# Second feed-forward stage of a fused attention kernel: groups of four pages taken in rounds of two

## What is computed

```
x = x + xattn(layernorm(x), ctx, ctx)        # 16 heads, causal
x = x + ffn_attn(layernorm(x))
# ffn_attn: q, k, v are each a "fast feed-forward" tree of the same input:
cur = 0                                       # 4 levels, 15 nodes, 16 leaves
for _ in range(4):
    cur = 2 * cur + 1 + (x . node_w[cur] + node_b[cur] >= 0)
leaf = cur - 15
y = relu(x @ w1[leaf] + b1[leaf]) @ w2[leaf] + b2[leaf]    # 256 -> 64 -> 256
# then softmax(q k^T / 16) v per batch
```

## Time and profile before

| | us |
|---|---|
| median of 3 executions | 640.76 (640.52 to 642.57) |
| profiled execution, its own time | 640.1 |
| its span in the profile | 638.3 |
| PE busy in the span | 586.1 (92%) |
| DVE / ACT / POOL busy | 439.1 / 299.0 / 236.9 |
| feed-forward stage, 425.3 to 551.8 | 126.5, PE busy 123.0, ACT 95.4, DVE 59.6, DMA share 0.97 |

### The profile page before, as it was taken

How to read it: one execution, slowest core, us unless ns; L and a number is a source line. 1 busy time by engine, 2 the same in 40 slices (tenths; PEclk the granted TensorE clock), 3 DMA queues, 4 the chain that set the end, 5 groups by cost and what they waited for, 6 DMA issues and landing times.

```text
span 638.3 us, 14744 instructions
## 1 busy us (share of the span) xinstructions
PE 586.1 (92%) x5131; PEld 494.5 (77%) x5131; DVE 439.1 (69%) x1511; ACT 299.0 (47%) x482; POOL 236.9 (37%) x298
## 2 busy tenths in 40 slices
PE   8677999999899999999999897859999999799996
PEld 7566888877788887888888686848888888689995
DVE  2765666988788898898898787873555555156664
ACT  4104544544444453554445355007877787533331
POOL 6700010143143243334323326660006666666551
PEclk9869999999899999999999899879999999999999
DMA  6798788898998898899898749977999999766653
GB/s 190 221 305 261 237 230 226 252 260 238 283 271 249 286 310 247 258 297 283 251 296 275 208 134 303 309 254 274 324 364 387 411 408 375 258 191 197 200 177 126
DMA packets 99639, 169.58 MB, mean 266 GB/s; under 512 B 12848, under 2 KB 67824, under 8 KB 99568
## 3 DMA queue, kind: packets, MB, share of 16 engines
q1 hardware_dynamic: 87712, 141.83, 70.5%
q0 software_dynamic: 9216, 25.18, 12.5%
q10 hardware_dynamic: 2640, 1.65, 0.9%
HBM read 92.59 MB, written 75.50 MB: 263 GB/s over the span
## 4 chain that ended last, share of the span: by engine, by line
PE 51%; DMA 26%; SPq 13%; DVE 5%; issue 3%; ACT 1%; POOL 1%; DVEq 0%; ACTq 0%; POOLq 0%
DMA parts_dram<-k_lo 9%; DMA k<-parts_dram 8%; PE banks L840 6%; PE banks L825 6%; PE banks L814 6%; DMA parts_dram<-q_lo 5%; SPq L334 5%; PE banks L882 4%; PE banks L903 4%; PE banks L530 4%; PE banks L545 4%; PE banks L557 3%; SPq L317 2%; PE banks L871 2%; PE banks L573 2%
## 5 line engine op out<-in xcount | busy, mean ns | idle before, releaser
L1537 POOL DMA_INDIRECT xs_dram<-xn2s,place x96 | 95.7, 997 | 159.4 <-ACT pt L936 142.4
L1174 DVE TENSOR_REDUCE mneg<-banks 128x2 f32<-128x512 f32 x240 | 121.8, 548 | 44.9 <-PE banks L546 43.8
L936 ACT ACTIVATE pt<-banks 128x768 f32<-128x768 f32 x128 | 103.5, 810 | 102.2 <-PE banks L558 101.7
L545 PE MATMUL banks<-k,q 107*128 107x256 f32 x240 | 76.4, 369 | 17.7 <-DMA k<-parts_dram 10.9
L557 PE MATMUL banks<-q,k 109*128 109x256 f32 x256 | 74.0, 341 | 2.0 <-DMA q<-m_lo 0.3
L545 PEld LDWEIGHTS banks<-k,q 107*128 107x128 f32 x240 | 46.5, 194 | 29.3 <-DMA k<-parts_dram 16.3
L558 PE MATMUL banks<-q,k 109*128 109x128 f32 x256 | 57.3, 224 | 0.0
L573 PE MATMUL banks<-pt,vp 128*32 128x256 f32 (+1 forms) x1024 | 56.4, 339 | 0.4 <-ACT pt L936 0.4
L1596 POOL DMA_INDIRECT q_all<-ys_dram,place x32 | 30.8, 964 | 67.1 <-DMA ys_dram<-yb 53.8
L546 PE MATMUL banks<-k,q 107*128 107x128 f32 x240 | 54.4, 227 | 0.0
L557 PEld LDWEIGHTS banks<-q,k 109*128 109x128 f32 x256 | 48.7, 190 | 6.8 <-ACT pt L936 5.7
(11 more groups left out here) (177 smaller groups left out, 1290.9 us busy)
## 6 DMA issues: line engine op xcount, KB each, us to landing
ys_dram<-yb SPq DMA_DIRECT2D x36, 512.0 KB, 6.2
xb<-xs_dram SPq DMA_DIRECT2D x35, 512.0 KB, 7.7
k<-parts_dram SPq DMA_DIRECT2D x128, 128.0 KB, 3.8
q<-parts_dram SPq DMA_DIRECT2D x64, 256.0 KB, 4.6
xs_dram<-zero SPq DMA_DIRECT2D x45, 256.0 KB
xs_dram<-zero SPq DMA_DIRECT2D x18, 384.0 KB, 4.8
tables<-leafw SPq DMA_DIRECT2D x16, 257.0 KB, 8.2
xt<-x SPq DMA_DIRECT2D x16, 256.0 KB, 4.9
```

What stands on the lines that cost most here:

```text
L545: mm(ps[:, 0:S], q[0:KN, t, P:S], k[0:KN, t, :], start=True, stop=True)
L936: nc.scalar.activation(pt[:, 2 * p:2 * p + 2, :], st_banks(b, p)[:, :, 0:S + P], ACT.Exp, scale=SC).then_inc(exp_sb, 1)
L1174: last = nc.vector.tensor_reduce(mneg[1 - u][:, t, 2 * j:2 * j + 2], S_BANKS[:, :, cols], axis=AX.X, op=ALU.max, negate=True)
L1537: gp.indirect_dma_start(xs_dram[tree], bass.IndirectOffsetOnAxis(ap=place[:, k:k + 1], axis=0), xn2s[m % RING][:, t, :], None).then_inc(sc ...
```

## The change

Quads are handled in rounds of two. On PE a round is now: transposes of q + 2 and q + 3, second layers of q and q + 1, first layers of q + 2 and q + 3 (before: one quad of each kind in turn). ACT and SP follow the same order: both `copy_xT`, both `copy_y`, both `relu`; two loads, two stores. The transposes alternate between `pairs[0]` and `pairs[1]`, and the first layers move to banks 4 and 5, which the second layer of even quads uses too; so `block_h` waits for the `copy_y` of the even quad before it, and `block_out` waits for both `relu` of the round. POOL's gathers are released by `after_sixth`, six points in a round of two. No instruction of the computation is added or taken away.

```
--- before.py
+++ after.py
@@ -483,12 +483,14 @@
                     scattered(sp, tree, m)
             for q in range(QB, QB + AHEAD):
                 load_quad(q)
-            for q in range(TREES * QUADB):
-                if q + QB + AHEAD < TREES * QUADB:
-                    load_quad(q + QB + AHEAD)
-                store_quad(q)
-                if q in TABLE2:
-                    load_table(2, 2 + TABLE2.index(q))
+            for q in range(0, TREES * QUADB, 2):
+                for ahead in (q + QB + AHEAD, q + QB + AHEAD + 1):
+                    if ahead < TREES * QUADB:
+                        load_quad(ahead)
+                for done in (q, q + 1):
+                    store_quad(done)
+                    if done in TABLE2:
+                        load_table(2, 2 + TABLE2.index(done))
 
 
             def rows(ap, b):
@@ -806,30 +808,30 @@
                     pe.wait_ge(xb_first, 16)
                 else:
                     pe.wait_ge(xb_in[w], 16 * (q // QB + 1))
-                ge(pe, xbT_sb, q)
+                ge(pe, xbT_sb, q - 1)
                 for m in range(4):
                     if q == 0 and m == 2:
                         pe.wait_ge(xb_in[0], 16)
                     for c in range(C):
-                        last = nc.tensor.transpose(banks[c][:, m * P:m * P + P], xb[w][:, m, c * P:c * P + P], ident[:])
+                        last = nc.tensor.transpose(pairs[w % 2][:, c, m * P:m * P + P], xb[w][:, m, c * P:c * P + P], ident[:])
                 last.then_inc(xbT_ps, 1)
 
             def block_h(q):
 
                 pe.wait_ge(xbT_sb, q + 1)
                 pe.wait_ge(w_cp, 8 * (q + 1))
-                ge(pe, h_sb, 2 * (q - 1))
+                ge(pe, y_sb, 2 * (q // 2) - 1)
                 for r in range(2):
                     for c in range(C):
                         for e in range(2):
-                            last = mm(banks[2 + q % 2][e * HID:(e + 1) * HID, r * P:r * P + P],
+                            last = mm(banks[4 + q % 2][e * HID:(e + 1) * HID, r * P:r * P + P],
                                       wb1[(2 * q + r) % UP][:, e, c * HID:c * HID + HID], xbT[q % 2][:, c, 2 * e + r, :],
                                       start=(c == 0), stop=(c == C - 1))
                 last.then_inc(h_ps, 1)
 
             def block_out(q):
 
-                pe.wait_ge(h_sb, 2 * (q + 1))
+                pe.wait_ge(h_sb, 4 * (q // 2 + 1))
                 ge(pe, y_sb, q - 1)
                 if q == 0:
                     pe.wait_ge(b2_sb, 2 * TREES)
@@ -848,12 +850,16 @@
             block_T(0)
             block_T(1)
             block_h(0)
-            for q in range(Q):
+            block_h(1)
+            for q in range(0, Q, 2):
                 if q + 2 < Q:
                     block_T(q + 2)
-                if q + 1 < Q:
-                    block_h(q + 1)
+                    block_T(q + 3)
                 block_out(q)
+                block_out(q + 1)
+                if q + 2 < Q:
+                    block_h(q + 2)
+                    block_h(q + 3)
 
             pe.wait_ge(y_sb, Q)
 
@@ -1027,14 +1033,14 @@
 
                 act.wait_ge(xbT_ps, q + 1)
                 ge(act, h_ps, q - 1)
-                nc.scalar.copy(xbT[q % 2][:].rearrange("p c m k -> p c (m k)"), pairs[0][:]).then_inc(xbT_sb, 1)
+                nc.scalar.copy(xbT[q % 2][:].rearrange("p c m k -> p c (m k)"), pairs[q % 2][:]).then_inc(xbT_sb, 1)
 
             def relu(q):
 
                 act.wait_ge(h_ps, q + 1)
                 ge(act, y_ps, q - 1)
                 for r in range(2):
-                    nc.scalar.activation(hT[q % 2][:, r, :], banks[2 + q % 2][:, r * P:r * P + P], ACT.Relu,
+                    nc.scalar.activation(hT[q % 2][:, r, :], banks[4 + q % 2][:, r * P:r * P + P], ACT.Relu,
                                          bias=wb2[(2 * q + r) % UP][:, D:D + 1]).then_inc(h_sb, 1)
 
             def copy_y(q):
@@ -1047,12 +1053,16 @@
             copy_xT(0)
             copy_xT(1)
             relu(0)
-            for q in range(Q):
+            relu(1)
+            for q in range(0, Q, 2):
                 if q + 2 < Q:
                     copy_xT(q + 2)
-                if q + 1 < Q:
-                    relu(q + 1)
+                    copy_xT(q + 3)
                 copy_y(q)
+                copy_y(q + 1)
+                if q + 2 < Q:
+                    relu(q + 2)
+                    relu(q + 3)
 
 
             def copy_qT(i, u):
@@ -1596,22 +1606,22 @@
                 gp.indirect_dma_start(rows_all[:, t // T, (t % T) * D:(t % T) * D + D], None, ys_dram[tree],
                                       bass.IndirectOffsetOnAxis(ap=place[:, m:m + 1], axis=0)).then_inc(done, 16)
 
-            def after_third(e):
-
-                q, third = e // 3, e % 3
-                if third == 0:
-                    gp.wait_ge(y_ps, q)
-                elif third == 1:
-                    gp.wait_ge(xbT_ps, min(q + 3, TREES * QUADB))
+            def after_sixth(e):
+
+                q, sixth = e // 6 * 2, e % 6
+                if sixth < 2:
+                    gp.wait_ge(xbT_ps, min(q + 3 + sixth, TREES * QUADB))
+                elif sixth < 4:
+                    gp.wait_ge(y_ps, q + sixth - 1)
                 else:
-                    gp.wait_ge(h_ps, min(q + 2, TREES * QUADB))
+                    gp.wait_ge(h_ps, min(q + sixth - 1, TREES * QUADB))
 
             taken = 0
             for tree, rows_all, done, count in ((0, q_all, q_in, NB * T), (1, k_all, k_in, KB * T)):
                 for s in range(QB):
                     gp.wait_ge(y_out[s], 16 * (tree + 1) * QUADB // QB)
                 for t in range(count):
-                    after_third(3 * GATHER_FROM + taken * 3 * (TREES * QUADB - GATHER_FROM) // ((NB + KB) * T))
+                    after_sixth(3 * GATHER_FROM + taken * 3 * (TREES * QUADB - GATHER_FROM) // ((NB + KB) * T))
                     gather_row(tree, t, rows_all, k_late[(t // T - KFIRST) // 2] if tree == 1 and t >= KFIRST * T else done)
                     taken += 1
             def late_row(n):
```

## The result

The changed kernel takes 634.8 us (median of 6 executions, 632.1 to 638.4). The kernel before, timed again beside it, took 642.5 (6 executions, 640.5 to 647.2), 1.7 more than the 640.8 of its first three. The ratio of the two is 0.989 (95% interval 0.986 to 0.992), and 0.993 (0.989 to 0.997) when both were timed once more (12 and 35 executions). The gain is clear of no change, and by the two intervals lies between some 2 and 9 us. The profiled execution took 635.9 us, 4.2 less than the profiled one of before, and its span is 634.1. Executions differ by some us in the first stage, which the change does not touch, so the feed-forward stage is read from its own rows.

What follows compares the result with a forecast made beforehand. PE bounds the kernel through what it issues plus 0.57 us of gaps per quad, with DMA nearly second bound. PE's -7.3 us plus DMA's 1.6 give -5.7, from 640.8 to 635.1 us; 80% range 632.3 to 639.0.

Steps and rivals of the forecast that it cites:

- the handover from ACT costs more: Rival, chance 0.17: drain after the ACT wait, or ACT 0.12 late; round 6.40 to 6.45, DMA doesn't bind, 636.6 us.
- A gap belongs to the change of shape; six per round become three: PE, feed-forward stage: array-shape changes cause the gaps; per round of two, 0.57 us of gaps instead of 1.14.
- The first layer waits for `copy_y`, 0.10 beyond the gap: PE's first layers stand behind ACT's copy through shared banks 4 and 5: 0.10 us extra per round, bounds 0 and 0.27.
- Round 6.23: Feed-forward stage: a round of two quads takes 6.23 us against 6.69 before, 0.46 less.
- DMA takes back 1.6 us: Gather part, second half: PE waits for late loads; loss 1.2 to 3.0 us, taken as 1.6.
- then DMA was mis-sized: Sign of being wrong: no transposes wait for a transfer in the feed-forward stage.
- the carry: DMA queue enters the gather part fuller, draining 0.60 instead of 0.83 per quad before it: some 2 us more landing time.
- First round at 434.2: Start of the feed-forward stage: after both first layers, the second at full clock, the first round starts at 434.2 us.
- End of the stage, weights, gathers, third stage: Third stage starts at 544.5 instead of 551.81, length unchanged at 86.5 us; DVE's weights cost 0, gathers 0, at most 0.5.
- DMA has enough room: Rival, chance 0.20: landing times stay under the room and 417 GB/s need not be the ceiling; 633.5 us.
- a slower kernel: Rival, chance 0.10: loads and stores in twos collide, the DMA rate falls from 413 to 355 GB/s; 644.7 us.

Runs made afterwards that it cites:

- the two dummies: Changed kernel plus one unneeded matmul between a round's transposes, on 64 or 128 array rows: rounds 6.61 to 6.63 or 6.42 to 6.43 us, against 6.36.
- own banks: Changed kernel with first layers in banks 2 and 3, waiting for both transposed-page copies instead of `copy_y`: round 6.19 us, ratio to the kernel before 0.994.
- more to move: Changed kernel plus one unneeded 131 KB transfer with each load from quad 4 on: quad 0's first layer to third stage 124.5 us, against 115.1.
- the ones without gathers: The own banks kernel with POOL's 50 gathers put off until PE finished the stage: rounds 6.19 us, one of 6.63 after the table loads.
- 64-row dummy: Changed kernel plus one unneeded 16-column matmul on 64 array rows ahead of odd quads' transposes: rounds 6.61 to 6.63 us before the gathers, against 6.36.

## Why the prediction was right, and where it was not

The time (635.1 forecast, 634.8 measured) and the direction were right. Beside the profiled execution, where the working belongs, 634.4 was forecast and 635.9 came: -4.2 instead of -5.7 us. That is the time of the rival "the handover from ACT costs more" (-4.2), not of the forecast. Step by step:

- *A gap belongs to the change of shape; six per round become three.* Right, shown by the two dummies. Inside a pair there is no gap.
- *The first layer waits for `copy_y`, 0.10 beyond the gap.* Right in kind, 0.14 in size (0.37 against 0.23). The profile does not name this wait (it reads "issue", where the prediction looked for ACT `yb`); the variant with own banks shows it. PE started 0.11 behind the end of the first copy in the round above (502.09 + 1.01 = 503.10, then 503.21), not the 0.05 of the earlier trace rows.
- *Round 6.23.* It is 6.36. The mis-sized terms, by the round above: transposes of a pair 1.73 (1.71 forecast), first layers 1.76 (1.70), and PE's start behind the copy's end 0.11 (0.05). The rest of the chain came as forecast: `copy_y` starts 1.41 behind the second layer's start and takes 1.01. The second layers are longer too, 2.17 instead of 2.14, but they lie beside that chain and cost nothing. The groups were summed from single-quad rows without the few hundredths between one block and the next. 17 rounds make that 2.2 us, the largest error.
- *DMA takes back 1.6 us.* Wrong for this kernel: no load was late in the stage, which is one of the prediction's own signs of being wrong ("then DMA was mis-sized"). The ceiling was right (some 415), and so was the mechanism, as the kernel with own banks and the one with more to move show. Landing times rose to 10.1, not 12.4. One step that failed is the carry, "some 2 us more": loads issued about 480 us landed in 6.6, about 0.5 above before, as the queue still drained between tables and gathers. The other is the round: at 6.36 a quad takes 3.18 us, so that its 3.23 of DMA work add 0.05 per quad and not 0.11, by an estimate 0.8 us over 16 quads instead of 1.8. The slower round also gives more room, 11.6 instead of 11.3. Even at nearly the forecast's pace, with own banks, DMA took back 0.7 us in one profile and 0.5 in the other (late loads of 0.24 + 0.42, and of 0.46), not 1.6.
- *First round at 434.2.* It was 435.18: quad 1's load landed 0.3 later, and the granted clock rose from 0.50 to 1.00 at 434.8 (433.3 in the profile before; I had taken 433.15), so that quad 1's first layer ran at half clock nearly to its end (both first layers 3.14 us). Another 1.0 us.
- *End of the stage, weights, gathers, third stage.* From the last round's start to the third stage 4.3 us, as forecast; the third stage is unchanged in length.

So two errors against the kernel (2.2 and 1.0 us) stood against one in its favour (1.6), and the scatter of executions did the rest: the medians differ by 7.7 us (642.5 and 634.8), the profiled executions by 4.2. That the median fell within 0.3 us of the forecast is luck. "DMA has enough room" (633.5) was in the end the rival that described DMA. "The handover from ACT costs more" was partly so, with a third of its price. Nothing spoke for a slower kernel: pairs of loads did not lower the rate (412 to 414 GB/s in 500 to 535 us in three profiles of the changed kernel, 405 before).

## What to carry to other kernels

If PE is the bound and its waits read "issue" at the borders between steps, compare the array shapes on both sides: grouping steps of one shape removes the gaps, and takes banks so that they can be grouped; then check what now sits in the bank that the next step wants. Before such a gain is counted, work out what DMA must move per step and how many us of room a load has: here the 5% from 6.69 to 6.36 us per round was still free, and of the next 3%, to 6.19, the last one or two rounds were not. And count the start of such a stage too: there own banks lost what their rounds gained. And add up a group's length from rows of several blocks in a row, not from one block times two.

## What the runs showed of the hardware that I had not expected

- The gap at a change of shape is not constant: 0.17 us behind groups of 128-column matmuls, 0.23 behind the second layer's 256-column ones, 0.02 behind a lone one of 16 columns. At half clock the 0.17 is 0.33. It looks like the time that the matmuls in flight still need; that is argued from these rows, not shown by itself.
- DMA holds 412 to 416 GB/s (512 KB loads and stores with gathers) over 35 us, with a share of 1.03, in all profiles but those of the kernel before, of the two dummies and of the ones without gathers, and no kernel got more over that stretch.
- In one batch of runs kernels of this family took some 25 us longer, and rounds of the gather part were 0.9 to 1.9 us too long, none without gathers. In 500 to 520 us the one with the 64-row dummy moved 357 GB/s, the one with more to move 413, so the rate that DMA can reach was no lower there. Thirteen minutes later, with the same chip number on record, the kernel before took 638.9 us again. The cause stays open.
